# Normalising in the last expert: output stored in the expert phase, the last expert's rows stored over by indirect transfer

## What is computed

```python
x = _layernorm(x + attention_and_experts_1(x))   # linear attention, then 8 experts with GELU
x = _layernorm(x + experts_2(x))                 # 8 experts, silu(g) * u
# experts_2: every token goes to its two best experts, an expert takes at most 1280 of them
gu = jnp.einsum('ecd,efd->ecf', xb, w12)
g, u = jnp.split(gu, 2, axis=-1)
h = jax.nn.silu(g) * u
yb = jnp.einsum('ecf,edf->ecd', h, w3).reshape(E * C, D)
...
out = jnp.zeros((T, D), x.dtype).at[tokens].add(ys)
```

## Time and profile before

| | us |
|---|---|
| timed runs, median of 3 (lowest, highest) | 1545.46 (1545.22, 1546.62) |
| the profiled run, its own time | 1548.21 |
| its span, first to last instruction | 1546.3 |
| TensorE busy | 1461.0 (94%) |
| VectorE busy | 1011.2 (65%) |
| ScalarE busy | 727.1 (47%) |
| GpSimd busy | 746.5 (48%) |
| last instruction of TensorE ends | 1519.6 |

### The profile page before, as it was taken

The page is one execution under the profiler, slowest core; times in us unless marked ns, Lnnn a source line. Parts: engine busy times, 40 slices in busy tenths (PEclk is TensorE's granted clock), DMA queues, the critical chain, the costliest instruction groups (busy, mean ns, idle before and its releaser), DMA issues. The chain is left out here.

```text
span 1546.3 us, 36023 instructions
## 1 busy us (share of the span) xinstructions
PE 1461.0 (94%) x11755; PEld 1419.0 (92%) x11755; DVE 1011.2 (65%) x2768; ACT 727.1 (47%) x1735; POOL 746.5 (48%) x749
## 2 busy tenths in 40 slices
PE   8999984999999999999949999999999999999993
PEld 7888864999999999999938999999999999999993
DVE  6999976667667667666565656565565655566455
ACT  4767653555455445545543334343433433344333
POOL 3677652566566566655523344433444334433433
PEclk9999995999999999999968999999999999999996
DMA  7122123244234243342613132413132131411117
GB/s 257 42 70 56 56 73 108 58 102 103 42 96 102 48 96 93 51 130 35 192 50 109 27 111 33 116 29 109 28 108 42 27 109 29 115 34 28 28 24 228
DMA packets 64547, 123.41 MB, mean 80 GB/s; under 512 B 14304, under 2 KB 52832, under 8 KB 61792
## 3 DMA queue, kind: packets, MB, share of 16 engines
q0 software_dynamic: 36416, 46.58, 18.4%
q1 hardware_dynamic: 28064, 76.02, 13.7%
HBM read 79.66 MB, written 42.90 MB: 79 GB/s over the span
## 5 line engine op out<-in xcount | busy, mean ns | idle before, releaser
L972 POOL DMA_INDIRECT acc<-ysb,IDX x160 | 258.8, 1617 | 132.4 <-ACT ysb L1074 66.3
L1111 DVE TENSOR_TENSOR E_hraw<-E_sg,bank 128x256 f32<-128x256 f32 x320 | 134.5, 420 | 282.7 <-ACT E_sg L1042 214.2
L965 POOL DMA_INDIRECT E_mg<-meta,IDX x160 | 151.0, 943 | 335.6 <-DVE E_gate L1095 308.4
L1166 PE MATMUL bank<-E_xT,ws 128*128 128x256 f32 x960 | 272.2, 284 | 5.1 <-DVE E_xT L1086 5.0
L1167 PE MATMUL bank<-E_xT,ws 128*128 128x256 f32 x960 | 271.5, 283 | 0.0
L1168 PE MATMUL bank<-E_xT,ws 128*128 128x256 f32 x960 | 271.3, 283 | 0.0
L1122 DVE TENSOR_TENSOR E_hT<-E_hraw,E_hT 128x256 fp32r<-128x256 f32 x640 | 259.9, 416 | 0.0
L1118 DVE CAST E_hT<-E_hraw 128x256 fp32r<-128x256 f32 x640 | 208.0, 325 | 62.1 <-ACT E_hraw L1045 40.2
L1042 ACT ACTIVATE E_sg<-bank 128x256 f32<-128x256 f32 x320 | 121.6, 384 | 256.3 <-PE bank L1168 243.4
L1166 PEld LDWEIGHTS bank<-E_xT,ws 128*128 128x128 f32 x960 | 183.0, 191 | 6.3 <-issue 5.8
L1166 PE MATMUL bank<-ws,E_hT 128*128 128x256 f32 x640 | 183.8, 287 | 0.0
(11 more groups left out here) (207 smaller groups left out, 3940.6 us busy)
## 6 DMA issues: line engine op xcount, KB each, us to landing
wraw<-in_w_ffn SPq DMA_DIRECT2D x8, 3072.0 KB, 10.7
wraw<-in_w_moe SPq DMA_DIRECT2D x8, 2048.0 KB, 13.0
X<-acc SPq DMA_DIRECT2D x16, 512.0 KB, 5.4
acc<-x SPq DMA_DIRECT2D x32, 128.0 KB, 1.7
xn<-xn SPq DMA_DIRECT2D x32, 128.0 KB, 1.7
acc<-X POOLq DMA_DIRECT2D x4, 1024.0 KB, 8.3
acc<-X SPq DMA_DIRECT2D x8, 512.0 KB, 2.7
out<-C_xo SPq DMA_DIRECT2D x8, 512.0 KB, 5.6
```

Of the source, the lines that this page charges most:

```text
L965: nc.gpsimd.indirect_dma_start(out=mg[:, j, :], out_offset=None, in_=meta_dram, in_offset=at_slots(u, j)).then_inc(s_gm, 16)
L972: nc.gpsimd.indirect_dma_start(out=acc_dram, out_offset=at_slots(u, j), in_=ysb[:, j, :], in_offset=None, compute_op=ALU.add).then_inc(s_y ...
L1111: V.tensor_tensor(hraw[:, f % RING, :], sg[:, f % RING, :], bank[f % RING][:, UW:2 * UW], ALU.mult).then_inc(s_hm, 1)
L1166: nc.tensor.matmul(out, wh, mh, start=first, stop=False)
```

## The change

`final_phase` is gone. Its work is done inside the second layer's expert phase, while the last expert is computed (LAST_U = 35, units 35 to 39).

Once the scatters of units 0 to 34 have landed, SP loads X from `acc2` in three spans of 11, 11 and 10 tiles. At that moment the rows of tokens that aren't in the last expert are final. VectorE measures a span behind each of the units 35, 36 and 37 (`measure`). GpSimd computes one over the root by a power of −0.5 (`normal`: addition of eps, power, then a tensor_scalar for each tile, in place) and SP stores the spans to the output.

Of the tokens of the last expert these rows are wrong, since its share is missing. For them the last expert no longer scatters: GpSimd gathers their old rows from `acc2` to z, a view of the free wraw (`old_rows`), VectorE adds the unit's ysb and measures them (`add_old`), GpSimd normalises them (`normal` again) and, when the three stores of X have landed, stores them over by an indirect transfer to the output's rows (`put_rows`). For this VectorE turns the rows of IDX into tokens (`tokens_of_slots`, OIDX); empty entries go to 1280 rows behind the output's 4096, which the host cuts off. In the last unit VectorE takes the results directly from PSUM, with ScalarE for the root alone (`finish`).

The first four units of the last expert are written out one by one instead of as a loop, on every engine, so that the steps above can stand between them. At the start of the second layer's expert phase GpSimd sets six small buffers.

```diff
-                with eng.Fori(0, UPE - 1) as c:
-                    unit(e, c, e * UPE + c, s, width, True)
+                if last and glu:
+                    for c in range(UPE - 1):
+                        unit(e, c, e * UPE + c, s, width, True)
+                else:
+                    with eng.Fori(0, UPE - 1) as c:
+                        unit(e, c, e * UPE + c, s, width, True)
...
+            if glu:
+                sp.wait_ge(s_ys, 16 * UT * LAST_U)
+                for k, (a, b) in enumerate(F_SPANS):
+                    if k > 0:
+                        sp.wait_ge(s_tg, LAST_U + 1 + k)
+                    sp.dma_start(X[:, a:b, :], by_partition(acc_dram)[:, a:b, :]).then_inc(s_ldx[k], 16)
+                for a, b in F_SPANS:
+                    sp.wait_ge(s_xp, b)
+                    sp.dma_start(rows_out[:, a:b, :], X[:, a:b, :]).then_inc(s_out, 16)
+                sp.wait_ge(s_out, 16 * len(F_SPANS))
+                sp.wait_ge(s_put, 16 * FIX)
...
+            def normal(rows, aggregated, done):
+
+                a, b = rows
+                pool.wait_ge(s_mv, aggregated)
+                nc.gpsimd.tensor_scalar(ve[:, a:b], mv[:, a:b, 1], EPS, None, ALU.add).then_inc(s_eps, 1)
+                roots[0] += 1
+                pool.wait_ge(s_eps, roots[0])
+                nc.gpsimd.tensor_tensor(rs[:, a:b], ve[:, a:b], mhalf[:, 0:b - a], ALU.pow).then_inc(s_rs, 1)
+                pool.wait_ge(s_rs, roots[0])
+                for n in range(a, b):
+                    nc.gpsimd.tensor_scalar(row[n], row[n], mv[:, n, 0:1], rs[:, n:n + 1], ALU.subtract, ALU.mult).then_inc(done, 1)
...
+            def last_expert():
+                next_rows(LAST_U + 2)
+                pool.wait_ge(s_ys, 16 * UT * LAST_U)
+                pool.sem_inc(s_yf, 1)
+                pool.wait_ge(s_wl, 4 * E)
+                old_rows(0)
...
+                for k in range(2):
+                    normal(fix(k), FIX_AT[k], s_fix)
+                pool.wait_ge(s_out, 16 * len(F_SPANS))
+                pool.wait_ge(s_oi, 8)
+                for k in range(4):
+                    if k >= 2:
+                        normal(fix(k), FIX_AT[k], s_fix)
+                    pool.wait_ge(s_fix, (k + 1) * UT)
+                    for j in range(UT):
+                        put_rows(k * UT + j)
+                for j in range(UT):
+                    pool.wait_ge(s_last, j + 1)
+                    put_rows(4 * UT + j)
...
+            def add_old(k):
+
+                dve.wait_ge(s_old[(k + 1) // 2], 16 * UT * (1 if k == 0 else 2))
+                dve.wait_ge(s_yb, UT * (LAST_U + k + 2))
+                for j in range(UT):
+                    V.tensor_tensor(z[:, k * UT + j, :], z[:, k * UT + j, :], ysb[:, j, :], ALU.add).then_inc(s_z, 1)
+                dve.wait_ge(s_z, (k + 1) * UT)
+                dve.sem_inc(s_yf, 1)
+                measure(NT + k * UT, NT + (k + 1) * UT)
+
+            def finish(u):
...
+                    V.scalar_tensor_tensor(out=z[:, n, :], in0=b_y[j][:, 0:D], scalar=gate[:, u * UT + j:u * UT + j + 1], in1=z[:, n, :],
+                                           op0=ALU.mult, op1=ALU.add).then_inc(s_z, 1)
+                    dve.wait_ge(s_z, n + 1)
+                    measure(NT + n, NT + n + 1)
+                    dve.wait_ge(s_sd, j + 1)
+                    V.reciprocal(rs[:, NT + n:NT + n + 1], sd[:, j:j + 1]).then_inc(s_rc, 1)
...
+                    V.tensor_scalar(z[:, n, :], z[:, n, :], mv[:, NT + n, 0:1], rs[:, NT + n:NT + n + 1],
+                                    ALU.subtract, ALU.mult).then_inc(s_last, 1)
...
+                if glu and isinstance(u, int) and u >= LAST_U:
+                    k = u - LAST_U
+                    if k == 0:
+                        tokens_of_slots()
+                    else:
+                        add_old(k - 1)
+                    if k < len(F_SPANS):
+                        dve.wait_ge(s_ldx[k], 16)
+                        measure(*F_SPANS[k])
+                    if not more:
+                        finish(u)
```

More of the change, by code:

```diff
@@ L946, in _ @@
             next_weights(E - 1, 1, True)
[L948 to L951, removed]
+            if glu:
+                sp.wait_ge(s_ys, 16 * UT * LAST_U)
[9 more added lines that the diff above has]
+            else:
+                sp.wait_ge(s_ys, 16 * UT * (UNITS - 1))
+                for g in range(HEAD):
+                    t = slice(g * G, (g + 1) * G)
+                    sp.dma_start(X[:, t, :], by_partition(acc_dram)[:, t, :]).then_inc(s_head[g], 16)
         @block.gpsimd
@@ L979, in _ @@
+            roots = [0]
+            if glu:
+                for k in range(UPE):
+                    nc.gpsimd.memset(apart[:, k * UT:(k + 1) * UT], float(k * UT * P)).then_inc(s_half, 1)
+                nc.gpsimd.memset(mhalf[:, :], -0.5).then_inc(s_half, 1)
+                pool.wait_ge(s_half, UPE + 1)
             if kept:
@@ L989, in _ @@
                 pool.wait_ge(kept["plus"], 16 * NT // 8)
-            for u in range(UNITS):
+            for u in range(LAST_U if glu else UNITS):
                 if u + 2 < UNITS:
@@ L1056, in unit @@
                                          ACT.Copy).then_inc(s_wh, 1)
+                if glu and not more:
+                    nc.scalar.activation(warm[:, :], cst[:, C_EPS:C_EPS + 1], ACT.Sqrt)
+                    for j in range(UT):
+                        n = NT + FIX - UT + j
+                        act.wait_ge(s_mv, n + 1)
+                        nc.scalar.activation(sd[:, j:j + 1], mv[:, n, 1:2], ACT.Sqrt, bias=cst[:, C_EPS:C_EPS + 1]).then_inc(s_sd, 1)
+                    return
                 act.wait_ge(s_gt, u + 1)
                 act.wait_ge(s_yf, u + 1)
[L1059 to L1064, removed]
+                if glu:
                     act.wait_ge(s_y, u + 2)
@@ L1465, in build @@
         ys = [ctx.enter_context(nc.semaphore(f"ys{i}")) for i in range(2)]
-        head = [[ctx.enter_context(nc.semaphore(f"head{i}{g}")) for g in range(HEAD)] for i in range(2)]
+        head = [ctx.enter_context(nc.semaphore(f"head{g}")) for g in range(HEAD)]
         X = sb("X", [P, NT, D])
```

172 lines of the change are left out of this document (82 added, 90 removed).

## The result

The changed kernel takes 1551.42 us (median of 8 runs, 1550.06 to 1554.98), the kernel before beside it 1545.34 (8 runs, 1543.28 to 1547.05). The ratio is 1.0045, with a 95% interval of 1.0036 to 1.0055: slower by 0.45%, some 7 us (the medians lie 6.1 apart). The forecast was 1532.0, in a range of 1526.5 to 1541.0; the time lies above the range and on the other side of no change. The rival with the nearest number is the third, 1551.6.

The account below looks back on a forecast made before the run. TensorE bounds until 1519.6, then a 26.7 us tail, which the change removes. GpSimd's chain B, with 0.6 us of memsets, ends the span at 1532.8 instead of 1546.3: 1545.46 − 13.5 = 1532.0, range 1526.5 to 1541.

Parts of the forecast that it names:

- chain B: GpSimd's gathers, normalisations and stores in a row during the last expert; sets the end, span ending at 1532.8.
- the power: GpSimd's root step in normalising X: 1.6 to 3.3 us for 11 columns, 2.4 taken.
- the store: GpSimd's plain indirect store to the output: between a gather (1.3 us) and the accumulating scatter (1.9); 1.3 taken.
- the break-even of 1.10 a tile: GpSimd's 40 normalised tiles: 13.5 us to lose, 0.34 a tile; from 1.10 us a tile on the change loses.
- rival 4: Ten indirect stores on GpSimd cost the scatter's 1.9 us: 6 us more, 1538; tail of the forecast's 0.50.
- rival 1: GpSimd and VectorE miss each other, 0.54 a tile; unit 38's pair, stores end the span: 1527.2, chance 0.20.
- Rival 3: GpSimd shut out by the lock in its 40 tiles; at 1.25 us a tile 1551.6, slower; chance 0.06.
- the prediction's signs of a wrong sum: End chain from TensorE straight through VectorE, indirect store over 1.3 us, or 11-column power far from 2.4.
- The lock: GpSimd and VectorE shut each other out over shared ports: 0.22 us a GpSimd tile, 0.46 a VectorE operation.
- Rival 2: VectorE becomes the bound, 22.6 us in a unit of 17.5, through lock waits: 1537.3, chance 0.19.
- chain A: Last two slots on VectorE after the last matmul, 2.3 us, then store and landing: floor 1525.1; 5.7 us slack.

Follow-up runs that it names:

- forms: Kernel before, with another pair of operations for GpSimd's two tiles in each of the 8 groups of final_phase: 1545.52 us in its one run.
- after: The changed kernel itself, against the kernel before: 1551.42 us, ratio 1.0045.
- form: Changed kernel, GpSimd normalising by mult and add (scale and shift), not subtract and mult, with two more small operations a call: 1532.33 us, ratio 0.9930.
- add_mult: Changed kernel, GpSimd negating the mean and normalising by add and mult, one more small operation a call: 1534.13 us, ratio 0.9912.
- form_again: The kernel of form run once more, beside the kernel before on another occasion: 1538.56 us, ratio 0.9935.
- rows_first: Changed kernel, unit 38's rows fetched after 8 of 11 tiles and unit 39's after 2, not behind them: 1551.13 us, ratio 1.0050.

## Why the prediction was wrong, point by point

**The step that failed** is "Normalising a tile of 256: four in 2.16, so 0.54 each". The row is of line 1424, (multiply, add); the diff shows line 1025 with (subtract, multiply). The two were taken for one kind of instruction, because engine, name and shape agree. By itself such a tile costs 1.21, more than twice as much, in forms and in after with VectorE at rest. No tensor_scalar of before on GpSimd subtracts; the only subtraction of 128 × 256 there is a tensor_tensor (line 334, 826 ns in the mean). So the price should have been bounded from both sides, as the prediction did for the power and the store, with the break-even of 1.10 a tile in between; the chance of "slower" then could not have been 0.06.

**The rest of chain B held.** From the statistics of the first span to the last store the forecast had the pieces in this order and with these durations; what differs (forecast, then measured): the first span of 11 tiles with its root 11.0, 17.6; the second 11.0, 17.4; the third 10.1, 16.5; two pairs 5.7, 7.9; the last two pairs 5.5, 7.2. That is 23.3 us more, all of it in tiles: the power of 11 columns took 2.15 and 2.41 where 2.4 was taken, eps and power of 2 columns 1.1 for 1.35. It begins 2.1 us before the forecast's 1453.5, because the phases ahead of the layer end 2.3 us earlier in this profile. 1530.3 + 23.3 − 2.1 is 1551.5, and the last store ends at 1551.2. The stores cost the gather's price, 0.96 to 1.10 and 0.30 between (1.3 taken, rival 4 falls), and land in 2.0 (2.1).

**With the price put right the forecast stands.** form gains 0.70% of before, 10.8 us (8 to 13). The forecast's 13.5, less 5.5 for the additional small operations, plus 40 × 0.07 because a tile took 0.69 and not 0.76, is 10.8. By the same sum add_mult, with one small operation a call (some 2.2 us) and 0.77 a tile, comes to a gain of 11; 13.6 and 12.1 were measured. That form's median is 1532.3 and the forecast 1532.0 is luck in part: the chip of that group ran before itself 2 us below the 1545.46. And the forecast holds only while TensorE isn't late: in form_again TensorE ends 9 us later than in form, counted from the first normalisation of the last expert, and there the chain of rival 1 ends last (the wait of 2.25 us).

**Rival 3** named the right number by the wrong mechanism. Its point of break-even, 1.10 a tile, was right, and 1.34 lies beyond it; but of the 0.80 above 0.54 only 0.13 is the neighbour, and 0.67 the operation. Had the cause been the lock, form would have been slow as well. That 1551.6 and 1551.42 agree is luck. None of the prediction's signs of a wrong sum pointed at the tile: the chain didn't go through VectorE, the store cost 1.3, the power 2.4; only the tiles of 0.7 to 0.8 that it wanted to see were missing.

**The lock** was sized at 0.22 a tile; what the units add to a tile is 0.13 to 0.22, and 0.16 beside subtractions alone. On VectorE it was put at 0.46 for each cast and subtraction, up to 5 us a unit. In the last expert of after the cast took 318 ns in the mean (299 before), the subtraction 424 (419), and that of the next rows 812 (693): 40 × 0.02, 40 × 0.005 and 4 × 0.12 make 1.5 us in the whole expert. Rival 2, which lived on that term, had no ground.

**TensorE** was to wait 1 to 4 us for VectorE. It waited 0.6 us for VectorE and 9.3 for ScalarE. The prediction had seen the path (rows of unit 39, "land at some 1493") and found it covered; with 6.5 us more in each span they came some 11 us later, and nothing covered that. rows_first shows that it was free all the same, because chain A, for which 5.7 us of slack were reckoned, had far more: VectorE's last instruction ended at 1533.2 and GpSimd came to its row at 1549.0. Chain A itself took 2.4 us from the last matmul's end at 1530.8 (2.3 forecast).

**At the start of the layer** the memsets take 0.83 us of the changed kernel's profile, from their start at 803.29 to that of the first gather at 804.12, where 0.6 was taken. (In before that gather stands at 805.55; the phases ahead of it differ by more than the memsets cost.)

## What to carry to other kernels

The price of an instruction belongs to its operations too, not only to engine, name and shape: before a duration is taken from a row, compare the operation arguments of that line with those of the new one, and where they differ treat the new one as not in the trace, with a bound on both sides. On GpSimd write a normalisation of such tiles as (x · r) + b or (x + (−m)) · r; both need no subtraction over the tile, and one or two small operations on the column of means pay for it many times over. When work is moved to an engine that then has no gap left, multiply its most frequent instruction by its count first: 40 times 0.67 us decided this case, and nothing else came near.

## What the runs showed of the hardware

- GpSimd's tensor_scalar on 128 × 256 float32, scalars from a column: multiply and add in either order 0.54 us; a pair with a subtraction 1.22; a single multiplication or subtraction 0.91. With constants: (multiply, add) 0.39, (subtract, multiply) 1.06. That one operation costs more than two had not been expected by any theory here. Why is open: no run tells what the engine does differently.
- Casts on VectorE delay GpSimd by 30 ns a tile; subtractions of two SBUF tiles delay it by 160. Against the last expert of before the casts themselves take some 170 ns more, the subtractions some 180.
- After TensorE's wait of 8.7 us its granted clock was lower for a while (0.91 in the stretch with the wait and 0.80 in the next, 1.00 before them). Without that wait, in rows_first, it stayed at 1.00 to the end. In after, single matmuls start 0.21 us apart at first behind the wait, and 0.12 from 1509.4 on, which are the two levels of 1.2 and 2.4 GHz:

```profile
1508.87 0.41 PE L1345 MATMUL bank<-ws1b,E_hT 128*128 128x256 f32 x1
1509.08 0.39 PE L1343 MATMUL bank<-ws1b,E_hT 128*128 128x256 f32 x1
...
1510.16 0.28 PE L1345 MATMUL bank<-ws1b,E_hT 128*128 128x256 f32 x1
1510.28 0.28 PE L1343 MATMUL bank<-ws1b,E_hT 128*128 128x256 f32 x1
```
